# Edge attributes go round eight units, and the bins of three gather layers are summed in PSUM

## What is computed

```python
edge_index = stack([src, dst])
x = layernorm(x + gnn0(x, edge_index))                # out[src] += (x @ W.T + b)[dst]
x = layernorm(x + gnn1(x, edge_index))                # z[dst] += x[src]; (1+eps) x + z; two-layer MLP; layer norm; relu
x = layernorm(x + gnn2(x, src, dst, edge_weight))     # z[src] += w * x[dst]; two linear layers, batch norm, relu
x = layernorm(x + gnn3(x, edge_attr_128, edge_index)) # attention over edges: h[src], h[dst] and edge_attr @ ew_W
```

## Time and profile before

| | us |
|---|---|
| median of 3 runs | 6711.77 |
| lowest, highest | 6668.48, 6715.77 |
| the profiled execution | 6697.6 |
| its span | 6695.8 |
| edge stage (first to last scatter of POOL) | up to 1437 |
| gathers of layers 0, 1, 2 begin | 1552.8, 2720.2, 3916.0 |
| gathers of layer 3 begin | 5289.9 |

### The profile page before, as it was taken

The page is one execution under the profiler, slowest core; times in us unless marked ns, Lnnn a source line. Parts: engine busy times, 40 slices in busy tenths (PEclk is TensorE's granted clock), DMA queues, the critical chain, the costliest instruction groups (busy, mean ns, idle before and its releaser), DMA issues. The chain is left out here.

```text
span 6695.8 us, 59788 instructions
## 1 busy us (share of the span) xinstructions
PE 3668.7 (55%) x13489; PEld 2668.1 (40%) x13489; DVE 3506.0 (52%) x11201; ACT 1539.5 (23%) x4647; POOL 3992.8 (60%) x4069
## 2 busy tenths in 40 slices
PE   4555555544555555465565545555556455556555
PEld 2343434422333333344444433343443344445444
DVE  5555555544444444455555544444445456666666
ACT  2111111100000000000000012222224345556555
POOL 7666666644666666566666646666661255566553
PEclk8787777765667666677777767777777777777777
DMA  2111111112333333233333323333330223233333
GB/s 82 42 48 43 43 43 46 43 39 67 99 95 99 99 95 99 77 95 98 95 98 96 97 67 92 91 91 92 92 91 27 76 82 85 84 87 90 85 88 60
DMA packets 257644, 522.16 MB, mean 78 GB/s; under 512 B 88394, under 2 KB 128798, under 8 KB 257316
## 3 DMA queue, kind: packets, MB, share of 16 engines
q0 software_dynamic: 179984, 423.92, 22.5%
q1 hardware_dynamic: 77331, 94.66, 4.8%
HBM read 483.72 MB, written 34.57 MB: 77 GB/s over the span
## 5 line engine op out<-in xcount | busy, mean ns | idle before, releaser
L1307 PE MATMUL ps<-ZT,xT 128*128 128x256 f32 x4704 | 1624.6, 502 | 1186.5 <-DVE ACC L1907 816.0
L716 POOL DMA_INDIRECT ZT<-table,meta_dst x1616 | 1551.2, 960 | 1143.9 <-issue 370.6
L716 POOL DMA_INDIRECT ZT<-table,meta_src x1568 | 1485.2, 947 | 874.8 <-issue 375.2
L1907 DVE TENSOR_TENSOR ACC<-ps,ACC 128x256 f32 x2352 | 999.3, 425 | 1522.4 <-remote 799.1
L1307 PEld LDWEIGHTS ps<-ZT,xT 128*128 128x128 f32 x4704 | 1131.8, 253 | 1665.3 <-issue 818.9
L661 POOL DMA_INDIRECT rec_src<-ZT x800 | 863.9, 1080 | 505.8 <-DVE ZT L1829 269.5
L1317 PE MATMUL ps<-ZT,xT 128*128 128x256 f32 x1664 | 587.0, 527 | 464.7 <-issue 461.6
L1317 PEld LDWEIGHTS ps<-ZT,xT 128*128 128x128 f32 x1664 | 446.4, 276 | 590.2 <-issue 486.9
L1823 DVE SCALAR_TENSOR_TENSOR meta_src<-ps,bc 128x256 f32<-128x256 f32 x800 | 291.4, 421 | 608.9 <-remote 488.2
L1260 PE MATMUL ps<-ewW,xT 128*128 128x256 f32 x1600 | 578.3, 464 | 0.0
L1259 PE MATMUL ps<-bias,ones 128*128 128x256 bf16 x800 | 257.4, 322 | 558.8 <-DVE ZT L1829 265.4
(11 more groups left out here) (436 smaller groups left out, 4362.5 us busy)
## 6 DMA issues: line engine op xcount, KB each, us to landing
ACC<-in_edge_attr SPq DMA_DIRECT2D x200, 240.0 KB
ZT<-table,meta_dst POOLq DMA_INDIRECT x1616
ZT<-table,meta_src POOLq DMA_INDIRECT x1568
rec_src<-ZT POOLq DMA_INDIRECT x800
table<-X SPq DMA_DIRECT2D x98, 128.0 KB
table<-ZT SPq DMA_DIRECT2D x49, 128.5 KB
X<-in_x SPq DMA_DIRECT2D x1, 6144.0 KB
table<-z SPq DMA_DIRECT2D x24, 256.0 KB
```

Source lines behind the costliest of these rows:

```text
L716: pool.indirect_dma_start(rows[:, s % depth, 0:width], None, table[layer], bass.IndirectOffsetOnAxis(ap=ids[:, s, 0:1].bitcast(I32), axis= ...
L1307: nc.tensor.matmul(slot_sum(j), sel[:, k % 2, j, :], ring[:, (2 + k) % RG * G + j, 0:D], start=True, stop=True).then_inc(sem["summed"], 1)
L1907: v.tensor_tensor(dst, slot_sum(j), dst, ALU.add).then_inc(sem["added"], 1)
```

## The change

Two things are changed together, and some semaphores are merged to make room for them.

*Attributes.* Eight units go round in place of four. The other four lie in buffers that are idle in the edge stage: `cslot`, `tile_src` and two parts of `meta_dst`. SP waits for `pay_ready` of the unit eight before.

*Sums.* The 17 products of a bin go into two halves of PSUM, one for each of the bin's two tiles, accumulated there: the first product into a half opens it, the others add to it. Which half a slot belongs to is known at run time only: `order_tiles` writes 0 or 1024 (an offset in PSUM) to the tables in place of the tile, for all slots but the first, and PE loads 7 or 8 of these into registers for each group and addresses its matmuls with them. Bins use two pairs of halves in turn, in banks 0 and 2, and 1 and 3. Two bf16 products with zeros close a bin. DVE adds the two halves of a bin to `ACC` after every second group. `summed` and `added` count to the same numbers as before.

*Semaphores.* `scattered` is one in place of four, `stats_may` and `act_may` become `may`; neither changes who waits for what.

```diff
-AR = 4
+AR = 8
+HOMES = 4
...
+        lent = [cslot[:, 0:n], tile_src[:, 0:n].bitcast(F32)]
+        lent += [meta_dst[:, h * n // 2:(h + 1) * n // 2, :].rearrange("p s f -> p (s f)") for h in (1, 2)]
...
             load_attr(0, 0, AR)
...
-            load_attr(0, AR, ES)
             with sp.Fori(1, SITERS) as i:
-                load_attr(i, 0, AR)
+                load_attr(i, 0, ES // 2)
                 store_first(i - 1)
-                load_attr(i, AR, ES)
+                load_attr(i, ES // 2, ES)
...
                 first = 1 if k % 2 == 0 else 0
                 wait(pe, *ring_filled(layer, r, k))
                 wait(pe, sem["sel_ready"], g + (layer * GROUPS + 1))
+                b = bin_of(r, k)
+                halves = bin_sums(b)
+                _, past = nc.values_load_multi_w_load_instructions(
+                    (tile_src, tile_dst, tile_src)[layer][0:1, b * (BIN + 1) + 1 + first + (1 - first) * G:
+                                                          b * (BIN + 1) + 1 + (2 - first) * G],
...
                 if first:
-                    wait(pe, sem["cross_ready"], bin_of(r, k) + (layer * T + 1))
-                    wait(pe, sem["added"], n - BIN)
-                    nc.tensor.matmul(cross_sum, sel_x[:, :], ring[:, (2 + k) % RG * G, 0:D], start=True,
-                                     stop=True).then_inc(sem["summed"], 1)
+                    wait(pe, sem["cross_ready"], b + (layer * T + 1))
+                    wait(pe, sem["added"], layer * SUMS + (b - 1) * (BIN + 1))
+                    nc.tensor.matmul(halves[1], sel_x[:, :], ring[:, (2 + k) % RG * G, 0:D], start=True,
+                                     stop=False).then_inc(sem["summed"], 1)
                 for j in range(G):
-                    if j % 2 == 0:
-                        wait(pe, sem["added"], n + j - (G - 2))
-                    nc.tensor.matmul(slot_sum(j), sel[:, k % 2, j, :], ring[:, (2 + k) % RG * G + j, 0:D],
-                                     start=True, stop=True).then_inc(sem["summed"], 1)
+                    opens = first and j == 0
+                    into = halves[0] if opens else psf[:, bass.ds(past[j - first] + (b % 2) * 512, D)]
+                    mm = nc.tensor.matmul(into, sel[:, k % 2, j, :], ring[:, (2 + k) % RG * G + j, 0:D],
+                                          start=bool(opens), stop=False)
+                    if first or j < G - 1:
+                        mm.then_inc(sem["summed"], 1)
+                if not first:
+                    nothing = zero16[:, 0:1].to_broadcast([P, D])
+                    nc.tensor.matmul(halves[0], ones16[:, :], nothing, start=False, stop=True)
+                    nc.tensor.matmul(halves[1], ones16[:, :], nothing, start=False, stop=True).then_inc(sem["summed"], 1)
...
             v.memset(attr[96:P, :, :, :], 0.0).then_inc(sem["zeroed"], 1)
+            for home in lent:
+                v.memset(home[96:P, :], 0.0).then_inc(sem["zeroed"], 1)
...
+                rest = bin_tile[n][:, :, 2:]
+                link(v.tensor_tensor(rest, rest, bin_tile[n][:, :, 1:2].to_broadcast([P, T, BIN - 1]), ALU.not_equal))
+                link(v.tensor_scalar(rest, rest, float(2 * 512), None, ALU.mult))
...
             def accumulate(layer, r, k):
-                first = 1 if k % 2 == 0 else 0
-                into = registers((tile_src, tile_dst, tile_src)[layer], sums_until(0, r, k), G + first)
-                n = sums_until(layer, r, k)
-                if first:
-                    dst = ACC[:, bass.ds(into[0], D)]
-                    wait(dve, sem["summed"], n + 1)
-                    wait(dve, sem["added"], n)
-                    v.tensor_tensor(dst, cross_sum, dst, ALU.add).then_inc(sem["added"], 1)
-                for j in range(G):
-                    dst = ACC[:, bass.ds(into[first + j], D)]
-                    if j % 2 == 0:
-                        wait(dve, sem["summed"], n + first + slot_done(j, j))
-                    wait(dve, sem["added"], n + first + j)
-                    v.tensor_tensor(dst, slot_sum(j), dst, ALU.add).then_inc(sem["added"], 1)
+                b = bin_of(r, k)
+                n = layer * SUMS + b * (BIN + 1)
+                other_tile, own_tile = registers((tile_src, tile_dst, tile_src)[layer], b * (BIN + 1), 2)
+                halves = bin_sums(b)
+                dve.wait_ge(sem["summed"], n + BIN + 1)
+                wait(dve, sem["added"], n)
+                dst = ACC[:, bass.ds(own_tile, D)]
+                v.tensor_tensor(dst, halves[0], dst, ALU.add).then_inc(sem["added"], 1)
+                dve.wait_ge(sem["added"], n + 1)
+                dst = ACC[:, bass.ds(other_tile, D)]
+                v.tensor_tensor(dst, halves[1], dst, ALU.add).then_inc(sem["added"], BIN)
...
-                    accumulate(layer, r, k)
+                    if k % 2 == 1:
+                        accumulate(layer, r, k)
```

82 lines of the change are left out of this document (46 added, 36 removed).

## The result

The changed kernel takes 6663.0 us (median of 5 runs, 6655 to 6677), the kernel before 6698.5 (5 runs, 6668 to 6716): a ratio of 0.9948, 95% interval 0.9924 to 0.9972. That is a gain of 36 us where 350 were forecast; it lies inside the range (6230 to 6690), near its upper end, and in the case "no change" (6640 to 6700). The profiled span is 6671.0 us against 6695.8.

What follows compares the result with a forecast made beforehand. A PE-VectorE hand-over loop with late PE signals was taken to bound layers 0 to 2. 6695.8 + 1.8 - 300 - 40 - 20 + 4.7 + 1.8 = 6344 us; with 14 us for the median, 6360; range 6230 to 6690.

Steps and rivals of the forecast that it cites:

- no change: Layers 0 to 2: sums reach VectorE no sooner, selection waits instead, only tails and attributes gain; 6640 to 6700 us, chance 0.12.
- What bounds the layers: Layers 0 to 2: the PE-VectorE hand-over loop, not an engine's work, costs 0.19 to 0.20 us a slot, 150 us a layer.
- The floor: GpSimd's gathers: 0.95 us held plus 0.30 us of issue, so 1.25 us a slot when nothing is waited for.
- The 8.1 us: Start of layer 0: time from the end of PE's records to VectorE's next addition, taken as lateness of PE's word.
- The loop's sum of 17.1 against 20.0 us: Two groups: late word 8.1, selection 1.22, register load 2.1, PE's group 5.7 us, against GpSimd's issue of 16 slots.
- term of 300 us: Layers 0 to 2: gain from fewer stops, at 1.28 us a slot in layer 0, 1.33 in 1 and 2; ends 0 and 448.
- the late word lasts as long as GpSimd issues: Layers 0 to 2: stops let word through, one for 16 slots instead of about 8; 6450 up to 6580 us, chance 0.20.
- The tail: Ends of three layers: PE follows GpSimd by one to two groups, saving 13 us each, 40 us in all (0 to 60).
- The edge stage: Edge attributes: eight units let SP load four units earlier, saving 20 us (ends 0 and 58).
- One semaphore for the scatters in place of four costs nothing: Edge stage: merging the scatters' semaphores was costed at nothing, since it is waited for once.
- Register loads on PE: Each group on PE: loading 7 or 8 registers takes 2.1 us, bounds 0.6 and 8.1; it decides from 4.3 us.
- The closing matmuls: PE, two a bin, 294 in all: 0.64 us a bin, 95 us in all, hidden under GpSimd's issue.

Runs made afterwards that it cites:

- b_sums_group: The kernel before with only the sums in PSUM and one PE signal a group, attributes and scatter semaphores as before: 6523.9 us against 6585.1 (0.9927).
- b_ahead: The kernel before with sums in PSUM, signals once a group (layer 3: a pair), GpSimd held to three groups ahead in layer 0, two in layer 2: 6641.7 us.
- b_best: The kernel before with only the sums in PSUM, signals once a group (layer 3: once a pair): 6636.3 us against 6702.3 (0.9896).
- b_pair: The kernel before with PE signalling sums every second slot of layers 0 to 2, 8 signals a bin for 17: 5568.2 us against 5570.2 (0.9997).
- b_attr_only: The kernel before with only the attributes' part (eight units, new load order, shared semaphores), sums as before: 5587.5 us against 5570.2 (1.0031).

## Why the prediction was wrong, point by point

**What bounds the layers: wrong, and this is the step that failed.** The prediction read the 0.18 to 0.20 us a slot over the floor as the price of a loop between PE and VectorE, with a late signal of a constant 8.1 us in it, because both engines had idle time and the waits carried PE's name. The floor was right: 1.25 us, and in the prompt condition layers 0 to 2 stand on it. The excess isn't set by the loop's work. In layers 0 to 2 it comes to some 0.18 us for each gather that GpSimd issues (0.17 on chip 7), and it stays so when VectorE's additions go, when PE signals 2 or 17 times a bin, when GpSimd may be 16, 24 or 32 gathers ahead, when PE has 408 or 716 us of work in 1000, and when half the bytes move. The signal that lets GpSimd go on comes at the end of such a stop; others arrive while it still issues (at 1768.61 above). The 8.1 us was one reading at one place; in the changed kernel the same step takes 11.9 and 33.6 us. The loop's sum of 17.1 against 20.0 us rested on it, so nearly the whole term of 300 us went. The layers gave 0.1, 5.3 and 5.1 us, 10.5 in all. Of the signs that the prediction named, PE's long bursts came (16 records in 6.03 us) and the gathers didn't: 698 where 780 were forecast.

**The rival that came nearest** was "the late word lasts as long as GpSimd issues" (0.20), with 6450 us or more. Its stops are seen in every late trace, but it gave the stop a fixed length and so halved the loss when stops come half as often. The stop grows with the gathers before it, so fewer stops are longer ones: 86 of 1.5 us in layer 0 before, 33 of 4.0 in b_sums_group, 48 of 2.9 in layer 2 of b_ahead, together 130, 133 and 141 us. "No change" (0.12) had the time right, and what it said of the page came: the selection waits in the place of the additions, there are 86 stops in layer 0 before and after, and the tails gain. It put this down to a hand-over in each group, which the later runs don't bear out, so its hit is in part luck.

**The tail: right.** 40 us were forecast for three tails, 13 each; the gaps behind layers 0, 1 and 2 are 12.5, 10.6 and 8.2 us shorter, 31 in all. Behind the last gather of layer 0 PE has two groups left to sum where it had three: the last one runs from 2701.19 to 2707.14 us, 26 us behind the layer's last gather (2681.15), where it was 36 us behind before (2706.9 and 2670.7); GpSimd's idle time is 26.07 us, near the 25 forecast:

```profile
2701.19 5.95 PE L1327 MATMUL ps<-ZT,xT 128*128 128x256 f32 x16 [9.15 <-issue]
```
In the prompt condition the gaps behind layers 0 and 1 are 2.0 and 2.4 us longer with the change.

**The edge stage: wrong in sign.** 20 us gained were forecast. The eight units are worth a few us at most in either condition. PE's transposes have no wait for a DMA left in their groups (3.0 us of idle time before them, where 18.1 stood), as forecast, and no scatter came earlier for it. The first scatter is issued 2.1 us later (79.8, before 77.7), near the 1.8 put down for the memsets. "One semaphore for the scatters in place of four costs nothing: it is waited for once" is the wrong step: seven stops of about 3 us, 20 us in all. The forecast priced a semaphore by its waits; this cost sits on the issuing side.

**Register loads on PE: right.** The group's load takes 598 ns at least, 1702 in the median and 2494 at most (196 of them on tile_src), between the prediction's 0.6 and 2.1 us but for 31 of all 294 loads, and well under the 4.3 us from which they would decide:

```profile
L1314 PEldq TENSOR_LOAD <-tile_src x196: 598/1702/2494, 1574.9 to 5030.2; - x196
```

**The closing matmuls: right.** 0.27 us each and hidden; PE didn't become the bound even with 716 us of work in 1000.

**What stays open.** What in the machine needs 1.43 us for a gather in the late condition, and why a chip is in it at one time and not at another (chip 9 was in both), no run here shows. Nor do they show why PE's signals are late with it, while PE starts 1.0 us after VectorE's addition. Shown for layers 0 to 2 is what it isn't: the number of signals (2 or 17 a bin), PE's work, PE's instructions, the gather's bytes and rows, and GpSimd's distance ahead. That a little spacing doesn't come free (1151 in place of 1120 us) isn't explained, and a rate for each gather alone wouldn't give it; nor is layer 3, with its 1.61 us a gather.

**The version to keep.** b_best, the sums without the attributes' part, is 1.0 and 1.2% ahead of the kernel before in the late condition (0.9896 and 0.9878), and is 13 us below the changed kernel beside it (6636.3 and 6649.2 us), with intervals that overlap. It wasn't run in the prompt condition, where the sums' part costs about 10 us and nothing that ran was ahead of the kernel before (b_pair is level with it). No version ran that is ahead of the kernel before in both.

## What to carry to other kernels

A wait names who released it, not what set its length: before pricing a stop as someone's latency, plot its length against what was issued since the last one. Total stops per stage that stay equal under different programs point to a rate, and none of the re-ordered hand-overs here bought it back. A resource shared "because nobody waits for it" still has a price where it is used, so cost it there or try it alone.

## What the runs showed of the hardware that I had not expected

- The kernel before took 5570 us and 6585 to 6715 us, on one and the same chip (9) 5570 and 6702. In the first case a bin of PE's sums is added 0.14 us after PE's record ends; in the second up to 33.6 us after while GpSimd issues gathers, and a hand-over from PE takes 0.13 us where it issues none.
- In the slower case each GpSimd gather of layers 0 to 2 costs 1.42 to 1.45 us in the long run: 1.251 from gather to gather and 0.17 to 0.18 of later stop with 128 rows, 1.204 and 0.23 with 64 rows.
- All scatters counted on one semaphore: GpSimd stands for 3.0 to 5.3 us after every 113 of them (b_attr_only); on two or four, 0.3 to 0.7 us the first time and then 0.3, the issue gap.
- A scatter issued beside VectorE's scan of 3.60 us takes 3.2 to 4.3 us in place of 0.96, in both conditions (24 of 800 in the kernel before and in b_pair); a second one of each round, near the addition of 1.82 us, mostly takes 1.9 us.

The Trainium skill (TensorE: Matmul & The Clock Gate, The cost: per-tile semaphore tail) says that an increment on the last matmul alone saves about 26 ns for each one dropped; for 15 fewer a bin that is an estimate of 0.4 us. No run here shows it: with them dropped the changed kernel went from 5597.1 to 5598.0 us, and in the late condition a signal's lateness was of another order.
